# An expert's last half chunk of up columns as rounded columns beside their rests, and ScalarE rounding the gated products

## The chip, the cores and the metric

One core of a Trainium2 chip. The metric is the device time of one execution in microseconds (us), the median of several runs.

## What is computed

64 x 64 rows of 512 numbers (4096 tokens) are mapped by one of 8 subject matrices, and the result x goes through a layer of eight experts and a shared one. Cut to what matters here:

```
h1 = einsum('nc,efc->enf', x, expert_fc1)      # 8 experts, 352 hidden, C = 512
h2 = einsum('nc,efc->enf', x, expert_fc2)
h  = silu(h1) * h2
out_e = einsum('enf,ecf->enc', h, expert_proj)
y = combine (two experts per token) of out_e
y = y + sigmoid(x @ shared_gate_w.T) * ((silu(s1) * s2) @ shared_proj.T)   # 1408 hidden
return x_in + y
```

All of it is 32-bit. The kernel gets its accuracy from three passes of rounded operands: a number is split into a rounded part (hi, type fp32r) and the rest (lo = raw - hi, rounded too), and a product is hi*hi + hi*lo + lo*hi.

## The kernel before

Tokens come in tiles of 128. A first stretch (up to some 413 us) maps the tokens, runs five of the eleven shared chunks on blocks of 512 tokens and computes the routing. A last stretch (from some 896 us) runs the other six shared chunks and adds everything up. Between them lie the experts, 39 steps (XT): 32 *whole* tiles of 256 gathered tokens and 7 *single* tiles of 128. The step after a single is always a whole tile and is written together with it (`single_and_whole`, 7 times, whole tiles with a plain stage order but another queue order on VectorE and ScalarE). Of the other 25 whole tiles the first has an order of its own (`gate_first`, `hidden_first`), the last is done together with the preparation of the last stretch, and 23 go through `whole_step`; I call those plain.

A whole tile on TensorE (PE), lines 1003 to 1055:
- Stage 1: three chunks of hidden units, FCH = 128, 128 and 96 wide. For chunk j `whole_chunk` runs the gate half (h = 0) and the up half (h = 1) over KC = 4 slices of C, three passes of 256 columns each: 24 passes, 72 in all. Both halves go to `bank_h[j]`, columns 0 to 255 and 256 to 511. PE starts chunk j when `ex.h_mul` says that the bank of the tile before is read.
- Stage 2, `expert_stage2` (L1024): PE waits for `ex.h_lo` to reach 3i+2 (the rests of chunks 0 and 1), runs 12 passes of 512 columns with eight transposes of the next tile's rows in between, waits for 3i+3 (chunk 2) and runs 6 passes.

```
for ks in ((0, 1), (2,)):
    pe.wait_ge(ex.h_lo, 3 * i + ks[-1] + 1)
    for r in range(2):
```

Beside it, in queues that each engine works through in the written order:
- ScalarE (ACT), `whole_step` L1321: per chunk two roundings of the next expert's weight pieces (`w_hi`, `wp_hi`; 7 pieces a tile), then the silu of the gate half (`expert_gate`, L1316, to `g_sb`); then the roundings `x_hi` of the next tile, and `keep_y` copies of `bank_o`.
- VectorE (DVE), `whole_step` L1749: per chunk the rests of the two weight pieces (`split_w`, L1743, to `w_lo`, `wp_lo`), then `hidden` (L1619): product of up half and `g_sb` into `h_sb` (L1623, `ex.h_mul`), rounding to `h_hi` (L1625), rest to `h_lo` (L1627, `ex.h_lo`); at the end the rests `x_lo` of the next tile (`rest_x`, L1633). PE starts the next stage 1 when `ex.x_lo` and the `ex.w_lo` of the four up pieces are there.
- SP loads an expert's weights two steps ahead, once all rests of the tile's pieces are done (`next_load`).

```
def hidden(f, n, j, fn, width, bank2, tok):
    dve.wait_ge(f.g_ready, n + 1)
    ... tensor_tensor(h_sb, bank2, g_sb, ALU.mult).then_inc(f.h_mul, 1)
    dve.wait_ge(f.h_mul, n + 1)
    ... tensor_copy(h_hi, h_sb).then_inc(f.h_hi, 1)
    dve.wait_ge(f.h_hi, n + 1)
    ... tensor_tensor(h_lo, h_sb, h_hi, ALU.subtract).then_inc(f.h_lo, 1)
```

Of the kernel before, what the change touches and what calls it, by code (L numbers as in the profile page):

```python
# [108 lines left out]
def build_program(nc, x, subj, cond_w, gates, ew12, ewp, sw12, swp, consts, out):  # L109
# [10 lines left out]
    with ctx:  # L120
# [675 lines left out]
        def _(pe):  # L796
# [258 lines left out]
            def single_up(i):  # L1055

                pe.wait_ge(ex.x_lo, 2 * (i + 1))
                pe.wait_ge(ex.w_lo, PIECES * i + KC)
                for h in range(2):
                    for k in range(KC):  # L1060
                        a = k * 2 * F + h * F

                        def small(pas, at=3 * k):
                            q = at + pas
                            if h == 0 and q < 2 * KC:
# [23 lines left out]
            def single_and_whole(i, g, loaded, loaded_next):  # L1089
# [103 lines left out]
        def _(act):  # L1193
# [253 lines left out]
        def _(dve):  # L1447
# [171 lines left out]
            def hidden(f, n, j, fn, width, bank2, tok):  # L1619
# [357 lines left out]
```

## Time and profile before

| | us |
|---|---|
| median of 3 runs (lowest, highest) | 1267.74 (1266.4, 1268.84) |
| profiled execution, its own time | 1266.22 |
| its span, first to last instruction | 1264.2 |
| PE busy | 1247.4 |
| DVE busy | 866.7 |
| ACT busy | 488.5 |

A busy PE is not PE at its peak, since passes overlap and their ends are modelled. The time of a pass is read from the distance of the starts, or from the chain of waits, which puts passes end to end.

### The profile page before, as it was taken

How to read it: one execution, taken by the hardware profiler on the slowest of the kernel's cores; microseconds unless marked ns; L12 is line 12 of the kernel's file. 1: busy time of each engine (PE TensorE's matmuls, PEld its weight loads, DVE VectorE, ACT ScalarE, POOL GpSimd, SP SyncE). 2: the span in 40 equal slices, each digit the busy share in tenths (PEclk: the TensorE clock that was granted, in tenths of full speed). 3: DMA queues.
4: the chain of work that ended last, by engine and by line, in shares of the span. 5: the costliest groups of instructions: out<-in, count | busy, mean ns of one | idle time of the engine just before them, and what ended most of it. 6: DMA issues, size and time to landing. Idle time of an engine off the chain costs nothing.

```text
span 1264.2 us, 20269 instructions
## 1 busy us (share of the span) xinstructions
PE 1247.4 (99%) x7006; PEld 1075.0 (85%) x7006; DVE 866.7 (69%) x1414; ACT 488.5 (39%) x821; POOL 292.3 (23%) x395
## 2 busy tenths in 40 slices
PE   7999999999999999999999999999999999999998
PEld 5788888888888999999999999999887787887887
DVE  4544554459654787787787777778778778778675
ACT  4322232221011566666666665556313314213211
POOL 3267874000001121221221222110231130030110
PEclk9999999999999999999999999999999999999999
DMA  8488887202215678678678686784796785885842
GB/s 302 143 295 293 292 311 250 91 35 100 100 57 189 227 268 293 220 267 290 221 269 288 220 281 219 263 293 161 268 352 199 274 258 168 290 250 175 289 136 100
DMA packets 110670, 284.29 MB, mean 225 GB/s; under 512 B 11570, under 2 KB 11698, under 8 KB 104850
## 3 DMA queue, kind: packets, MB, share of 16 engines
q1 hardware_dynamic: 73410, 186.51, 40.9%
q0 software_dynamic: 13872, 54.27, 13.8%
q10 hardware_dynamic: 23328, 42.74, 10.2%
q8 instruction: 34, 0.56, 0.2%
q14 instruction: 26, 0.21, 0.0%
HBM read 217.16 MB, written 66.32 MB: 224 GB/s over the span
## 4 chain that ended last, share of the span: by engine, by line
PE 92%; DMA 3%; DVE 3%; ACT 1%; issue 1%; SPq 1%; DVEq 0%; ACTq 0%
PE bank_h L870 43%; PE bank_o L870 27%; PE bank_h L1132 9%; PE bank_t L1132 6%; PE bank_t L860 2%; PE bank_t L870 2%; PE bank_t L811 1%; DMA rawp<-ewp 1%; PE bank_o L821 1%; DMA w_early<-late_up 1%; DMA rawp<-swp 1%; DMA x_lo<-late_up 0%; PE bank_h L821 0%; PE bank_h L803 0%; DVE rawp L1840 0%
## 5 line engine op out<-in xcount | busy, mean ns | idle before, releaser
L870 PE MATMUL bank_h<-x_hi,w_hi 128*128 128x256 f32 (+2 forms) x1096 | 348.7, 318 | 0.3 <-DVE x_lo L1633 0.3
L870 PE MATMUL bank_h<-x_hi,w_lo 128*128 128x256 f32 (+2 forms) x1096 | 342.7, 313 | 0.0
L870 PE MATMUL bank_h<-x_lo,w_hi 128*128 128x256 f32 (+2 forms) x1096 | 341.9, 312 | 0.0
L870 PEld LDWEIGHTS bank_h<-x_hi,w_lo 128*128 128x128 f32 (+1 forms) x1096 | 200.2, 183 | 12.6
L870 PEld LDWEIGHTS bank_h<-x_hi,w_hi 128*128 128x128 f32 (+1 forms) x1096 | 200.3, 183 | 12.2 <-issue 0.9
L870 PEld LDWEIGHTS bank_h<-x_lo,w_hi 128*128 128x128 f32 (+1 forms) x1096 | 200.3, 183 | 11.2
L870 PE MATMUL bank_o<-wp_hi,h_hi 128*128 128x512 f32 (+1 forms) x502 | 204.9, 408 | 0.1
L870 PE MATMUL bank_o<-wp_lo,h_hi 128*128 128x512 f32 (+1 forms) x502 | 203.9, 406 | 0.0
L870 PE MATMUL bank_o<-wp_hi,h_lo 128*128 128x512 f32 (+1 forms) x502 | 202.7, 404 | 0.0
L1743 DVE TENSOR_TENSOR w_lo<-raw,w_hi 128x704 fp32r<-128x704 f32 x156 | 132.4, 885 | 56.7 <-ACT w_hi L1194 56.7
L1194 ACT ACTIVATE w_hi<-raw 128x704 fp32r<-128x704 f32 (+1 forms) x168 | 126.7, 802 | 8.9 <-DMA rawp<-swp 6.4
L756 POOL COPY idx_stage<-token_of 128x2 int32 (+3 forms) x39 | 9.8, 251 | 496.4 <-PE bank_t L860 321.6
L1240 ACT ACTIVATE g_sb<-bank_h 128x512 f32<-128x512 f32 x40 | 23.9, 598 | 243.4 <-PE bank_h L870 243.4
L870 PEld LDWEIGHTS bank_o<-wp_hi,h_lo 128*128 128x128 f32 (+1 forms) x502 | 94.3, 188 | 22.7
L870 PEld LDWEIGHTS bank_o<-wp_lo,h_hi 128*128 128x128 f32 (+1 forms) x502 | 94.6, 188 | 21.0
L870 PEld LDWEIGHTS bank_o<-wp_hi,h_hi 128*128 128x128 f32 (+1 forms) x502 | 94.6, 188 | 18.9 <-DVE h_lo L1627 0.8
L1623 DVE TENSOR_TENSOR h_sb<-bank_h,g_sb 96x256 f32<-96x256 f32 (+1 forms) x136 | 67.9, 499 | 59.8 <-ACT g_sb L1240 37.5
L760 POOL DMA_INDIRECT rows<-xf_rows,idx_stage x71 | 86.7, 1221 | 59.4 <-issue 59.4
L1461 DVE COPY xt<-bank_t 128x512 f32<-128x512 f32 x28 | 19.3, 690 | 90.3 <-PE bank_t L811 72.8
L1319 ACT ACTIVATE g_sb<-bank_h 128x256 f32<-128x256 f32 (+1 forms) x96 | 36.8, 383 | 110.2 <-PE bank_h L870 110.2
L781 POOL DMA_INDIRECT rows<-slot_rows,slot_of x32 | 32.3, 1009 | 190.1 <-DVE res L1840 121.5
L860 PE MATMUL bank_t<-cst,rows 128*128 128x128 f32 x284 | 75.8, 271 | 0.0
(238 smaller groups left out, 2169.8 us busy)
## 6 DMA issues: line engine op xcount, KB each, us to landing
raw<-ew SPq DMA_DIRECT2D x39, 1408.0 KB, 7.4
rawp<-ewp SPq DMA_DIRECT2D x39, 512.0 KB, 8.0
w_early<-late_up ACTq DMA_DIRECT2D x69, 256.0 KB, 3.9
slot_rows<-res SPq DMA_DIRECT2D x32, 512.0 KB, 4.1
x_hi<-late_up ACTq DMA_DIRECT2D x46, 256.0 KB, 3.9
x_lo<-late_up ACTq DMA_DIRECT2D x46, 256.0 KB, 3.1
xt_in<-xf_transposed SPq DMA_DIRECT2D x11, 1024.0 KB, 7.7
late_up<-raw POOLq DMA_DIRECT2D x6, 1792.0 KB, 7.9
```

Of the source, the lines that this page charges most:

```text
L760: pool.indirect_dma_start(rows[:, s, :], None, xf_dram, bass.IndirectOffsetOnAxis(idx_stage[:, s:s + 1].bitcast(U32), 0),).then_inc(ex.row ...
L781: pool.indirect_dma_start(picks[u][:, k, :], None, slot_dram, bass.IndirectOffsetOnAxis(slot_of[:, k, t:t + 1].bitcast(U32), 0),).then_inc ...
L811: m = pe.transpose(bank[:, c * P:(c + 1) * P], rows[:, k % 4, c * P:(c + 1) * P], ident)
L860: m = pe.transpose(bank_t[r % 2][:, k * P:(k + 1) * P], source[:, k * P:(k + 1) * P], ident)
L870: mm = pe.matmul(dst, a, m, start=(first and i == 0), stop=(last and i == 2))
L1132: m = pe.matmul(bank[:, :], halves[w][:, k, :], x2[x][:, k, :], start=(first and k == 0 and i == 0), stop=(k == 1 and i == 2), skip_group_ ...
L1194: copy = lambda o, i: nc.scalar.activation(o, i, ACT.Copy)
L1240: nc.scalar.activation(g_sb[:, (j % 2) * BN:(j % 2 + 1) * BN], bank_h[2 * (j % 2)][:, :], ACT.Silu).then_inc(f.g_ready, 1)
L1319: nc.scalar.activation(g_sb[0:fn, j * TS:(j + 1) * TS], bank_h[j][0:fn, 0:TS], ACT.Silu).then_inc(ex.g_ready, 1)
L1461: nc.vector.tensor_copy(xt[:, k % 2, :, :], bank[:, :].rearrange("p (k t) -> p k t", k=KC)).then_inc(fxt_ready, 1)
L1623: nc.vector.tensor_tensor(h_sb[0:fn, g], bank2, g_sb[0:fn, g], ALU.mult).then_inc(f.h_mul, 1)
L1743: nc.vector.tensor_tensor(lo, raw, hi, ALU.subtract).then_inc(ex.w_lo, 1)
```

## The change

An expert's up columns are stored in another order, so that the last 64 of a row are the ones that are treated in a new way. In `w12_hi` each slice now has 64 columns more (`E_HI = 2 * F + FOLD`): behind the rounded last 64 columns lie *their rests*. One stationary operand of 128 columns is thus 64 rounded columns beside their 64 rests. Two passes, one with x_hi and one with x_lo, give in partitions 0 to 63 hi*x_hi + hi*x_lo and in 64 to 127 lo*x_hi + lo*x_lo; their sum is the product. That takes 2 passes for a slice and not 3, and 17 for a slice over the tile and not 18. The 32 up columns of chunk 2 that are left ride in the gate half, whose stationary operand grows from 96 to 128 columns; they come out in partitions 96 to 127 of the bank's first half.

For chunk 2 ScalarE therefore copies partitions 64 to 127 of the up half to `u_sb[0:64]`, does the silu, and copies partitions 96 to 127 of the gate half to `u_sb[64:96]`. VectorE adds the other 64 partitions to `u_sb[0:64]` and multiplies `u_sb` and `g_sb`. The weight rests have 640 columns for the four up pieces, and one instruction (4x64 columns) writes the folded rests, counted by `ex.w_lo`, so all waits on it go by RESTS = 8 a tile in place of 7. A single tile still runs three passes over all columns and multiplies in two instructions (32 and 320 columns).

In plain tiles and the first, ScalarE rounds the gated products (`expert_h_hi`), not VectorE. In plain tiles it rounds chunk j-1 behind the gate of chunk j, and VectorE subtracts chunk j-1 behind the product of chunk j; in the first tile both come behind the same chunk's product. In the 7 whole tiles beside a single, and in the last, VectorE does all three as before.

```diff
+FOLD = 64
+E_HI = 2 * F + FOLD
+UP_AT = F + FCH[2][1] - FOLD
+FOLD_AT = 2 * F - FOLD
...
+        u_sb = h_sb[:, 3 * TS:4 * TS]
...
+        RESTS = PIECES + 1
+
+        def folded_piece(u):
+
+            raw = raw12[:, u * E_UP:(u + 1) * E_UP].rearrange("p (k f) -> p k f", k=KC)
+            hi = w12_hi[:, u * KC * E_HI:(u + 1) * KC * E_HI].rearrange("p (k f) -> p k f", k=KC)
+            return raw[:, :, FOLD_AT:2 * F], hi[:, :, FOLD_AT:2 * F], hi[:, :, 2 * F:E_HI]
...
+                bank = bank_h[j][:, h * TS:(h + 1) * TS]
+                if (j, h) == (2, 1):
+                    for part, x in enumerate((ex_x_hi, ex_x_lo)):
+                        m = pe.matmul(bank, w12_hi[:, hi + FOLD_AT:hi + E_HI], x[:, k, :], start=(start and part == 0),
+                                      stop=(stop and part == 1))
+                    return m
+                f = FCH[j][0] + h * UP_AT
+                return product(bank, (w12_hi[:, hi + f:hi + f + P], w12_lo[:, lo + f:lo + f + P]),
...
             def whole_chunk(i, u, j):
                 at_least(pe, ex.h_mul, 3 * (i - 1) + j + 1)
+                if j == 2:
+                    pe.wait_ge(ex.w_lo, RESTS * i + KC + 1)
...
             def expert_gate(i, j):
                 fn = FCH[j][1]
                 act.wait_ge(ex.h_full, 3 * i + j + 1)
-                nc.scalar.activation(g_sb[0:fn, j * TS:(j + 1) * TS], bank_h[j][0:fn, 0:TS], ACT.Silu).then_inc(ex.g_ready, 1)
+                if j == 2:
+                    copy(u_sb[0:FOLD, :], bank_h[2][FOLD:P, TS:2 * TS])
+                gate = nc.scalar.activation(g_sb[0:fn, j * TS:(j + 1) * TS], bank_h[j][0:fn, 0:TS], ACT.Silu)
+                if j == 2:
+                    gate = copy(u_sb[FOLD:fn, :], bank_h[2][fn:P, 0:TS])
+                gate.then_inc(ex.g_ready, 1)
+
+            def expert_h_hi(i, j):
+                fn = FCH[j][1]
+                act.wait_ge(ex.h_mul, 3 * i + j + 1)
+                copy(h_hi[0:fn, j, 0:TS], h_sb[0:fn, j * TS:(j + 1) * TS]).then_inc(ex.h_hi, 1)
...
                     if not gate_first:
                         expert_gate(i, j)
+                        if j:
+                            expert_h_hi(i, j - 1)
+                if not gate_first:
+                    expert_h_hi(i, 2)
...
+            def expert_gated(i, j):
+                fn = FCH[j][1]
+                up = bank_h[j][:, TS:2 * TS]
+                if j == 2:
+                    dve.wait_ge(ex.g_ready, 3 * i + 3)
+                    nc.vector.tensor_tensor(u_sb[0:FOLD, :], up[0:FOLD, :], u_sb[0:FOLD, :], ALU.add).then_inc(ex.u_ready, 1)
+                    dve.wait_ge(ex.u_ready, i + 1)
+                    up = u_sb[0:fn, :]
+                gated(ex, 3 * i + j, j, fn, TS, up, j)
...
             def whole_step(i, u, hidden_first=False, row_tiles=2):
                 for j in range(3):
                     if hidden_first:
-                        expert_hidden(i, j)
-                    split_w(i + 1, 1 - u, (2 * j, 2 * j + 1))
+                        expert_gated(i, j)
+                        expert_rest(i, j)
+                    split_w(i + 1, 1 - u, (2 * j, 2 * j + 1), row_tiles == 1)
                     if not hidden_first:
-                        expert_hidden(i, j)
+                        expert_gated(i, j)
+                        if j:
+                            expert_rest(i, j - 1)
+                if not hidden_first:
+                    expert_rest(i, 2)
```

Where instructions stand, as the built program has them, each with its line, its tiles and what it waits for. First VectorE in a plain tile, from the product of chunk 1 (`bank_h1`) to the rests of chunk 2; before:

```order
L1623 TENSOR_TENSOR h_sb<-bank_h1,g_sb 128x256 [waits ex_g_ready]
L1625 CAST h_hi<-h_sb 128x256 [waits ex_h_mul]
L1627 TENSOR_TENSOR h_lo<-h_sb,h_hi 128x256 [waits ex_h_hi]
L1742 REGISTER_ALU
L1743 TENSOR_TENSOR wp_lo<-rawp,wp_hi 128x512 [waits ex_w_hi]
L1742 REGISTER_ALU
L1743 TENSOR_TENSOR wp_lo<-rawp,wp_hi 128x512 [waits ex_w_hi]
L1622 REGISTER_ALU
L1623 TENSOR_TENSOR h_sb<-bank_h2,g_sb 96x256 [waits ex_g_ready]
L1625 CAST h_hi<-h_sb 96x256 [waits ex_h_mul]
L1627 TENSOR_TENSOR h_lo<-h_sb,h_hi 96x256 [waits ex_h_hi]
```

and now:

```order
L1663 TENSOR_TENSOR h_sb<-bank_h1,g_sb 128x256 [waits ex_g_ready]
L1675 TENSOR_TENSOR h_lo<-h_sb,h_hi 128x256 [waits ex_h_hi]
L1796 REGISTER_ALU
L1799 TENSOR_TENSOR wp_lo<-rawp,wp_hi 128x512 [waits ex_w_hi]
L1796 REGISTER_ALU
L1799 TENSOR_TENSOR wp_lo<-rawp,wp_hi 128x512 [waits ex_w_hi]
L1808 REGISTER_ALU
L1809 TENSOR_TENSOR h_sb<-bank_h2,h_sb 64x256 [waits ex_g_ready]
L1663 TENSOR_TENSOR h_sb<-h_sb,g_sb 96x256 [waits ex_g_ready,ex_u_ready]
L1675 TENSOR_TENSOR h_lo<-h_sb,h_hi 128x256 [waits ex_h_hi]
L1675 TENSOR_TENSOR h_lo<-h_sb,h_hi 96x256 [waits ex_h_hi]
```

The roundings (CAST) are gone. The rest of chunk 1 (the last row but one, 128x256), which stood right behind chunk 1's product, now stands behind the sum (64x256) and the product (96x256) of chunk 2; in its old place is the rest of chunk 0.

ScalarE in the same plain tile, from the gate of chunk 1 to the first x rounding; before:

```order
L1319 ACTIVATE g_sb<-bank_h1 128x256 [waits ex_h_full]
L1194 ACTIVATE wp_hi<-rawp 128x512 x2
L1318 REGISTER_ALU
L1319 ACTIVATE g_sb<-bank_h2 96x256 [waits ex_h_full]
L1222 ISA
L1194 ACTIVATE x_hi<-bank_t0 128x4x128 [waits ex_t_done]
```

and now:

```order
L1346 ACTIVATE g_sb<-bank_h1 128x256 [waits ex_h_full]
L1219 ACTIVATE h_hi<-h_sb 128x256 [waits ex_h_mul]
L1219 ACTIVATE wp_hi<-rawp 128x512 x2
L1343 REGISTER_ALU
L1219 ACTIVATE h_sb<-bank_h2 64x256 [waits ex_h_full]
L1346 ACTIVATE g_sb<-bank_h2 96x256
L1219 ACTIVATE h_sb<-bank_h2 32x256
L1219 ACTIVATE h_hi<-h_sb 128x256 [waits ex_h_mul]
L1219 ACTIVATE h_hi<-h_sb 96x256 [waits ex_h_mul]
L1247 ISA
L1219 ACTIVATE x_hi<-bank_t0 128x4x128 [waits ex_t_done]
```

Chunk 2 has three instructions behind `ex_h_full` where it had one, and the roundings of chunks 1 and 2 follow them.

PE in the same tile, at the end of stage 1 (`bank_h2`) and the start of stage 2 (`bank_o0`); before:

```order
L870 MATMUL bank_h2<-x_hi,w12_hi 96x256
L870 MATMUL bank_h2<-x_lo,w12_hi 96x256
L870 MATMUL bank_h2<-x_hi,w12_lo 96x256
L1052 REGISTER_ALU
L1026 REGISTER_ALU [waits ex_rows0]
L1031 ISA [waits ex_o_kept,ex_w_lo]
L870 MATMUL bank_o0<-wp_hi,h_hi 128x512 [waits ex_h_lo]
```

and now:

```order
L1027 MATMUL bank_h2<-x_lo,w12_hi 128x256
L1027 MATMUL bank_h2<-x_hi,w12_hi 128x256
L1027 MATMUL bank_h2<-x_lo,w12_hi 128x256
L1027 MATMUL bank_h2<-x_hi,w12_hi 128x256
L1027 MATMUL bank_h2<-x_lo,w12_hi 128x256
L1077 REGISTER_ALU
L1051 REGISTER_ALU [waits ex_rows0]
L1056 ISA [waits ex_o_kept,ex_w_lo]
L887 MATMUL bank_o0<-wp_hi,h_hi 128x512 [waits ex_h_lo]
```

The passes of the up half alternate x_hi and x_lo over one stationary operand, 8 in all where there were 12. What PE asks for ahead of the first pass of stage 2 is what it asked for before. In the whole tile beside a single, VectorE has the sum ahead of chunk 2's product, rounding and rest, then two weight rests of 640 columns, the folded rest (4x64), and then the two x rests.

## Rows read from the trace of the kernel before

**Rows 1.** The page's engines: busy us (share of the span) and instructions.
```profile
PE 1247.4 (99%) x7006; PEld 1075.0 (85%) x7006; DVE 866.7 (69%) x1414; ACT 488.5 (39%) x821; POOL 292.3 (23%) x395
```
**Rows 2.** The page's chain that ended last, share of the span by engine.
```profile
PE 92%; DMA 3%; DVE 3%; ACT 1%; issue 1%; SPq 1%; DVEq 0%; ACTq 0%
```
**Rows 3.** Timeline of PE (start us, us, instruction): stage 1 to stage 2.
```profile
658.71 0.28 PE L870 MATMUL bank_h<-x_hi,w_lo 128*96 128x256 f32 x1
658.83 0.39 PE L870 MATMUL bank_o<-wp_hi,h_hi 128*128 128x512 f32 x1
```
**Rows 4.** Chain in order of time (start us, us, what): stage 1 of that tile.
```profile
650.44 8.55 PE bank_h L870 x72
```
**Rows 5.** Timeline of ACT, same tile: chunk 1, weight pieces, chunk 2.
```profile
656.19 0.39 ACT L1319 ACTIVATE g_sb<-bank_h 128x256 f32<-128x256 f32 x1 [1.11 <-PE bank_h L870]
656.47 1.14 ACT L1194 ACTIVATE wp_hi<-rawp 128x512 fp32r<-128x512 f32 x2
659.03 0.38 ACT L1319 ACTIVATE g_sb<-bank_h 96x256 f32<-96x256 f32 x1 [1.41 <-PE bank_h L870]
```
**Rows 6.** Timeline of DVE, same tile: chunk 0's rest, chunk 2.
```profile
654.55 0.42 DVE L1627 TENSOR_TENSOR h_lo<-h_sb,h_hi 128x256 fp32r<-128x256 f32 x1
654.89 1.69 DVE L1743 TENSOR_TENSOR w_lo<-raw,w_hi 128x704 fp32r<-128x704 f32 x2
...
659.44 0.42 DVE L1623 TENSOR_TENSOR h_sb<-bank_h,g_sb 96x256 f32<-96x256 f32 x1 [0.42 <-ACT g_sb L1319]
659.89 0.29 DVE L1625 CAST h_hi<-h_sb 96x256 fp32r<-96x256 f32 x1
```
**Rows 7.** Groups by line and form (busy us, mean ns), DVE, then ACT.
```profile
L1627 DVE TENSOR_TENSOR h_lo<-h_sb,h_hi 128x256 fp32r<-128x256 f32 x64 | 27.2, 425 | 2.2
...
L1623 DVE TENSOR_TENSOR h_sb<-bank_h,g_sb 128x256 f32<-128x256 f32 x64 | 27.1, 423 | 12.3 <-ACT g_sb L1319 11.0
...
L1194 ACT ACTIVATE wp_hi<-rawp 128x512 fp32r<-128x512 f32 x83 | 47.6, 621 | 6.2 <-PE bank_o L870 6.2
```
**Rows 8.** Timeline of DVE and PE: stage 1 after a single's neighbour.
```profile
744.22 1.28 DVE L1633 TENSOR_TENSOR x_lo<-bank_t,x_hi 128x512 fp32r<-128x512 f32 x2
...
745.05 0.39 PE L870 MATMUL bank_o<-wp_hi,h_lo 96*128 96x512 f32 x1
745.75 0.38 PE L870 MATMUL bank_h<-x_hi,w_hi 128*128 128x256 f32 x1 [0.31 <-DVE x_lo L1633]
```
**Rows 9.** Timeline of DVE and PE: the last whole tile's stage 2.
```profile
890.43 0.42 DVE L1627 TENSOR_TENSOR h_lo<-h_sb,h_hi 128x256 fp32r<-128x256 f32 x1
...
890.61 0.28 PE L870 MATMUL bank_h<-x_hi,w_lo 128*96 128x256 f32 x1
891.00 0.47 PE L870 MATMUL bank_o<-wp_hi,h_hi 128*128 128x512 f32 x1
```
**Rows 10.** Timeline of PE and DVE: stage 2 beside a single.
```profile
645.22 0.39 PE L870 MATMUL bank_o<-wp_hi,h_hi 128*128 128x512 f32 x1
...
648.89 0.40 PE L870 MATMUL bank_o<-wp_hi,h_hi 96*128 96x512 f32 x1
...
650.28 0.28 PE L870 MATMUL bank_h<-x_hi,w_hi 128*128 128x256 f32 x1
...
646.96 1.68 DVE L1743 TENSOR_TENSOR w_lo<-raw,w_hi 128x704 fp32r<-128x704 f32 x2
648.56 1.28 DVE L1633 TENSOR_TENSOR x_lo<-bank_t,x_hi 128x512 fp32r<-128x512 f32 x2
```
**Rows 11.** Busy time by stretch: us, PE, PEld, DVE, ACT, POOL, clock, DMA share, GB/s.
```profile
30.00:34.00 4.00, 2.08 (x13) 1.72 (x12) 3.27 (x6) 1.81 (x3) 1.78 (x4) 1.00 0.90 345
...
658.83:663.89 5.06, 5.06 (x29) 4.07 (x27) 3.30 (x7) 2.50 (x5) 1.10 (x2) 1.00 0.57 212
```
**Rows 12.** Timeline of PE: the wait in the first stretch.
```profile
33.38 0.47 PE L870 MATMUL bank_t<-w_hi,wp_hi 128*128 128x512 f32 x1 [1.92 <-DVE w_lo L1471]
```

More of the change, by code:

```diff
@@ L1004, in up_product @@
             def up_product(i, u, j, h, k, start, stop):
-                f0, fn = FCH[j]
-                a = u * E_UP + k * 2 * F + h * F + f0
-                return product(bank_h[j][0:fn, h * TS:(h + 1) * TS], (w12_hi[:, a:a + fn], w12_lo[:, a:a + fn]),
+                lo, hi = expert_up(u, k)
+                bank = bank_h[j][:, h * TS:(h + 1) * TS]
[6 more added lines that the diff above has]
+                return product(bank, (w12_hi[:, hi + f:hi + f + P], w12_lo[:, lo + f:lo + f + P]),
                                (ex_x_hi[:, k, :], ex_x_lo[:, k, :]), start, stop)
@@ L1325, in whole_step @@
                         expert_gate(i, j)
+                        expert_h_hi(i, j)
                     if j == 0:
@@ L1617, in slot_tokens, with gated @@
                 nc.vector.tensor_copy(token_of[:, :], tok_f[:, :]).then_inc(routing_done, 1)
-            def hidden(f, n, j, fn, width, bank2, tok):
+            def gated(f, n, j, fn, width, bank2, tok):
                 g = slice(tok * width, (tok + 1) * width)
@@ L1628, in hidden @@
                                         ).then_inc(f.h_lo, 1)
+            def hidden(f, n, j, fn, width, bank2, tok):
+                gated(f, n, j, fn, width, bank2, tok)
+                rounded(f, n, j, fn, width, tok)
+                hidden_rest(f, n, j, fn, width, tok)
             def rest_x(f, n, r):
@@ L1736, in _, with split_w @@
             hiddens(0, BLOCKS - 1, between=steps_of({0: slot_tokens}))
-            def split_w(i, u, part):
+            def split_w(i, u, part, single=False):
                 pieces = list(expert_pieces(u))
@@ L1742, in split_w, with expert_rest @@
                     dve.wait_ge(ex.w_hi, PIECES * i + k + 1)
-                    nc.vector.tensor_tensor(lo, raw, hi, ALU.subtract).then_inc(ex.w_lo, 1)
+                    if k < KC and not single:
+                        raw, hi, lo = (a[:, 0:FOLD_AT] for a in (raw, hi, lo))
+                    nc.vector.tensor_tensor(lo, raw, hi, ALU.subtract).then_inc(ex.w_lo, 2 if single and k == KC - 1 else 1)
+                    if k == KC - 1 and not single:
+                        raw, hi, lo = folded_piece(u)
+                        nc.vector.tensor_tensor(lo, raw, hi, ALU.subtract).then_inc(ex.w_lo, 1)
+            def expert_gated(i, j):
[7 more added lines that the diff above has]
+                gated(ex, 3 * i + j, j, fn, TS, up, j)
+            def expert_rest(i, j):
+                hidden_rest(ex, 3 * i + j, j, FCH[j][1], TS, j)
             def expert_hidden(i, j):
-                fn = FCH[j][1]
-                hidden(ex, 3 * i + j, j, fn, TS, bank_h[j][0:fn, TS:2 * TS], j)
+                expert_gated(i, j)
+                rounded(ex, 3 * i + j, j, FCH[j][1], TS, j)
+                expert_rest(i, j)
             def whole_step(i, u, hidden_first=False, row_tiles=2):
@@ L1772, in single_and_whole @@
                 dve.wait_ge(ex.h_full, 3 * (i + 1))
-                nc.vector.tensor_tensor(h_sb[:, 0:F], bank_h[2][:, 0:F], g_sb[:, 0:F], ALU.mult).then_inc(ex.h_mul, 3)
+                back = UP_AT - F
+                nc.vector.tensor_tensor(h_sb[:, F - back:F], bank_h[2][:, 0:back], g_sb[:, F - back:F], ALU.mult
+                                        ).then_inc(ex.u_ready, 1)
+                nc.vector.tensor_tensor(h_sb[:, 0:F - back], bank_h[2][:, back:F], g_sb[:, 0:F - back], ALU.mult
+                                        ).then_inc(ex.h_mul, 3)
                 split_w(i + 1, 1, (2, 3))
```

34 lines of the change are left out of this document (22 added, 12 removed).

## The prediction

> **What bounds the kernel now.** I read the page's engine table first: PE is busy for 99% of the span, VectorE (DVE) for 69% [rows 1]. The chain that ended last runs over PE for 92% [rows 2]. So any pass taken from PE counts in full, and any new wait of PE counts in full too. I then read the timeline of one plain whole tile. Stage 1 is 72 passes of 256 columns that take 8.55 us, 0.119 us each [rows 4]. Stage 2 follows with no gap: the last pass of chunk 2 starts at 658.71, the first of stage 2 at 658.83 [rows 3]. Before the change this works because VectorE finishes the hidden rests of chunks 0 and 1 (rounding and rest) while PE is still in stage 1; the rest of chunk 1 is issued ahead of the two 512-column weight rests, which are ahead of chunk 2's product. Only chunk 2's own rest comes late, and stage 2 asks for it only after its first 12 passes.
>
> **Passes removed.** The up half of chunk 2 needs 8 passes in place of 12. With 32 whole tiles that is 128 passes x 0.119 us = 15.2 us less on PE. The 20 remaining passes of chunk 2 grow from 96 to 128 stationary columns; chunks 0 and 1 already run 128 at the same 0.119 us on average over the tile, so I cost this at nothing (at most 0.4 us in all, if a 96-column pass were 0.0005 us shorter).
>
> **The wait added.** This is the main term. The order rows of VectorE show the rest of chunk 1 (128x256, waiting for ex_h_hi) now behind chunk 2's sum and chunk 2's product, and both of these wait for ScalarE (ACT), which waits for PE's last pass of chunk 2. PE's next instruction, the first pass of stage 2, waits for ex_h_lo at the count that this same rest of chunk 1 gives. PE does its work in order, so nothing else of PE fills the time. What I add up, from T, the moment at which PE would start stage 2 (658.83 in the tile read):
> - ScalarE sees the bank full at T+0.20 (659.03 against 658.83) [rows 3, 5]. Then three instructions in place of one: the copy of 64 partitions, the silu, the copy of 32 partitions. One of 256 columns out of a bank takes 0.38 us and lets the next start after 0.28 [rows 5]. The last ends at T+0.20+0.28+0.28+0.38 = T+1.14.
> - VectorE starts 0.03 later (659.44 after 659.41) [rows 5, 6], at T+1.17. The sum (64x256) is followed by the product after 0.45, as product and rounding follow each other now (659.44, 659.89): T+1.62. The rest of chunk 1 waits for nothing new and starts 0.34 later (654.55, 654.89): T+1.96. It takes 0.42 and ends at T+2.38 [rows 6].
> - ScalarE's rounding of chunk 1, which that rest needs, starts behind the three at about T+1.04. At a length between 0.38 (256 columns from a bank) and 0.62 (512 from SBUF) [rows 5, 7] it is done by T+1.7, before VectorE asks. Nothing for it.
> - PE starts again after the rest has landed. Two places show the price: after an x rest that ended at 745.50 PE started at 745.75, and its first pass took 0.10 longer than usual (0.38, not 0.28): 0.35 us [rows 8]. After the rest that ended at 890.85 it started at 891.00 with 0.08 more (0.47, not 0.39): 0.23 us [rows 9]. I take 0.30.
>
> So PE stands still for 2.38 + 0.30 = 2.7 us in each plain tile. There are 23: the 32 whole tiles without the 7 that share a step with a single, the first (its rests stay in place) and the last (all done by VectorE as before). 23 x 2.7 = **62.1 us**. Bounds: if ScalarE's two added copies cost only some 0.11 each in place of 0.28 and the restart 0.15, it is 2.2 us, 50.6 in all. If none of the six instructions overlaps its neighbour (0.10 more for two on ScalarE and for one on VectorE) and the restart is 0.35, it is 3.1 us, 71.3 in all.
>
> The product of chunk 2 reads SBUF where it read a bank. The rows say the same length for both, 425 ns for a 256-column subtraction in SBUF and 423 ns for the product out of a bank [rows 7]. The Trainium skill, VectorE: DVE Perf Modes, the section on the TRN2 errata, gives a bank source 62 cycles more than an SBUF source, 0.065 us; by it the sum would be 1.5 us lower (23 tiles), as an estimate from that page. The rows disagree, and I follow them.
>
> **Chunk 2's own rest in a plain tile.** ScalarE rounds it after the product (T+2.04), VectorE subtracts by about T+2.9. PE wants it 12 passes and 8 transposes after its restart, 3.67 us later (645.22 to 648.89) [rows 10]. Hidden, with 3 us to spare. The x rests behind it keep their distance to stage 2, because PE's transposes move with the stall.
>
> **The 7 whole tiles that share a step with a single.** There VectorE still does product, rounding and rest together, the rest of chunk 1 is long done, and stage 2 starts on time. But the rests of the next x tile wait in the same queue. Before: they start at 648.56, take 1.28 and end at 649.84, 4.62 after T = 645.22; PE needs them at 650.28, 5.06 after T [rows 10]. After: T+1.17 sum, +1.62 product, +2.07 rounding, +2.40 rest, +2.74 free. Two weight rests of 640 columns at 0.73 each (704 columns have 0.80: 646.96 to 648.56 for two, less some 1 ns a column), +4.20. The folded rest of 4x64 columns 0.34, +4.54. Two x rests 1.28, +5.82. With the restart of 0.35 PE starts stage 1 at T+6.2 and not T+5.06: 1.1 us, 7.7 us over seven; one of them already pays 0.5 now (745.75 in place of 745.28) [rows 8]. **+7.2 us**, between 4 (0.6 each) and 11 (1.6 each).
>
> **The rest.** The last whole tile starts stage 2 when VectorE has the rest of chunk 1 ready, at 890.85, already a little late now [rows 9]; VectorE has a queue of its own there, so the 0.5 us saved on PE is lost: +0.5. In the first tile ScalarE's rounding now waits for VectorE's product ahead of the weight copies; +0.5 (0 to 1.5). The 32-column piece cut from the single's product lies under 12 passes. SP and the DMAs wait for the same count of weight rests, one more per tile, and a tile that takes longer gives loads more room. Nothing.
>
> **Sum.** Against the profiled execution: 1266.2 - 15.2 + 62.1 + 7.2 + 1.0 = **1321.3 us**. That execution lies 1.5 us under the median of the three runs (1267.7), within their spread, and I don't correct for it. Low end: 1266.2 - 15.2 + 50.6 + 4.0 = 1305.6. High end: 1266.2 - 14.8 + 71.3 + 11.0 + 2.0 = 1335.7. I take 1304 to 1338. A difference of 0.2% (2.5 us) is about what a measurement of this kernel can tell from none.
>
> **Rivals.**
> 1. *The stall is covered* (faster). If the rest of chunk 1 were ready when stage 1 ends, only the passes and the smaller terms would be left: 1266.2 - 15.2 + 7.2 + 1.0 = 1259.2. This decides below a stall of 0.3 us a tile (7.0 / 23). For it: VectorE has 31% idle time and the product of chunk 1 is long done. Against it: the queue is in order, and the order rows put the rest behind two instructions that need PE's last pass. 0.03.
> 2. *The clock falls in the stalls* (much slower). A PE that stands still for 2.7 us in every 16 could be given the lower level, 1.2 GHz, when it resumes. If stage 2 then ran at half speed, its 5.06 us [rows 11] would become 10.1: 23 x 5.06 = 116 us more, 1437. Against it: after PE stood still for 1.92 us at 33.38 the granted clock stayed 1.00, the upper level of 2.4 GHz, in that stretch with half its time idle [rows 11, 12]. For it: that happened once, and shorter, and no row shows 2.7 us again and again. 0.07. The Trainium skill, TensorE: Matmul & The Clock Gate, the section on HAM oscillation, says that waits between bursts can bring the clock down at each burst; by that rule this rival's time would hold; the one row that bears on it does not agree.
> 3. *Part of the chain overlaps or part of the added work lies elsewhere* (a stall of 0.4 to 2.1 us, 1267 to 1304): 0.03, of which 0.01 within 0.2% of now. Something longer than my bounds (1338 to 1400): 0.03.
> 4. *The change does not do what it says*: the order rows show 8 passes, three ScalarE instructions and the rest behind the product. No chance given.
>
> My forecast has 0.84. Faster by over 0.2%: 0.03. Within: 0.01. Slower: 0.96.
>
> **What would show it.** In the profile after: PE's waits should list bank_o against DVE h_lo with about 60 us over 23 times, longest near 2.8; ScalarE's copy, silu, copy start 0.28 apart; VectorE's sum, product and rest of chunk 1 directly behind them; bank_h against DVE x_lo with some 7 times 1 us; PE's count falls by 128, its busy time by about 15 us; the granted clock stays at 1.00. A list of PE's waits without h_lo would make the forecast wrong, and so would a clock under 1.00. If h_lo waits are there but near 2.0 or 3.5 us, the chain is right and a length in it is off.

## The result, and the profile after

The changed kernel takes **1350.15 us** (median of 4 runs, 1348.32 to 1352.87), the kernel before 1267.61 us on the same chip (1266.4 to 1268.84): a ratio of 1.0661, 95% interval 1.0647 to 1.0676. The forecast was 1321.3, range 1304 to 1338. Slower was right; the time lies 29 us above the forecast and 12 above the range. The profiled execution took 1348.32 us, its span 1346.3.

The page's engines, the slices of PE's busy share and granted clock, and the chain by engine:

```profile
PE 1265.1 (94%) x6878; PEld 1077.7 (80%) x6878; DVE 859.4 (64%) x1413; ACT 540.6 (40%) x957; POOL 298.6 (22%) x395
...
PE   7999999999998988988989888888999999999999
...
PEclk9999999999999999999999998999999999999999
...
PE 85%; DVE 6%; ACT 3%; issue 2%; DMA 2%; POOL 1%; POOLq 0%; SPq 0%; DVEq 0%; ACTq 0%
```

PE has 128 instructions fewer than in [rows 1], yet 17.7 us *more* busy time, where the forecast had some 15 less. Fewer passes take longer in sum, which points at the clock, but not by itself: in the run with the late rests alone (below, clock 1.00 and no fold) PE's busy time is 1253.8, 6.4 us over the kernel before with the same passes. The chain now runs over DVE and ACT for 9% of the span, where [rows 2] had 4%. Who PE waits for (us in total, times, longest us), where the kernel before had none of the first and one of 0.3 us of the second [rows 8]:

```profile
PE bank_o L887 <- DVE h_lo L1675: 57.9, 24, 2.6
PE bank_h L887 <- DVE x_lo L1686: 8.3, 8, 1.1
```

The stall of a plain tile, in the timelines of ACT, DVE and PE (start us, us, instruction, idle before it and its releaser). It answers to [rows 3, 5, 6]; T, the moment at which PE would start stage 2, is here 471.84, 0.12 behind the start of the last pass:

```profile
472.04 0.38 ACT L1219 ACTIVATE h_sb<-bank_h 64x256 f32<-64x256 f32 x1 [0.67 <-PE bank_h L1027]
472.43 0.38 ACT L1346 ACTIVATE g_sb<-bank_h 96x256 f32<-96x256 f32 x1
472.82 0.38 ACT L1219 ACTIVATE h_sb<-bank_h 32x256 f32<-32x256 f32 x1
473.22 0.42 ACT L1219 ACTIVATE h_hi<-h_sb 128x256 fp32r<-128x256 f32 x1
...
473.23 0.42 DVE L1809 TENSOR_TENSOR h_sb<-bank_h,h_sb 64x256 f32<-64x256 f32 x1 [1.05 <-ACT h_sb L1219]
473.68 0.42 DVE L1663 TENSOR_TENSOR h_sb<-h_sb,g_sb 96x256 f32<-96x256 f32 x1
474.02 0.98 DVE L1675 TENSOR_TENSOR h_lo<-h_sb,h_hi 128x256 fp32r<-128x256 f32 x2
...
471.72 0.28 PE L1027 MATMUL bank_h<-x_lo,w_hi 128*128 128x256 f32 x1
474.49 0.50 PE L887 MATMUL bank_o<-wp_hi,h_hi 128*128 128x512 f32 x1 [2.49 <-DVE h_lo L1675]
```

The chain is the forecast one, link by link: three ScalarE instructions, the sum, the product, chunk 1's rest (the first of the two under `h_lo`), PE. ScalarE's three stand 0.39 apart, not 0.28. PE starts 2.65 after T, and its first pass is 0.11 longer than usual (0.50 against 0.39): 2.76 us a tile. Of the 23 plain tiles 22 have this stop of 2.49 us; the first has 2.58.

The rest of the surprise is in PE's restarts. The identical stop of 2.49 us is followed in some tiles by a pass of 0.50 and in others by one of about 0.80. (A first pass of 0.50 does not yet say that the clock held: behind 854.27, 871.81 and 940.23 it falls up to 1 us later.)

```profile
474.49 0.50 PE L887 MATMUL bank_o<-wp_hi,h_hi 128*128 128x512 f32 x1 [2.49 <-DVE h_lo L1675]
490.46 0.79 PE L887 MATMUL bank_o<-wp_hi,h_hi 128*128 128x512 f32 x1 [2.49 <-DVE h_lo L1675]
...
854.27 0.50 PE L887 MATMUL bank_o<-wp_hi,h_hi 128*128 128x512 f32 x1 [2.49 <-DVE h_lo L1675]
871.81 0.50 PE L887 MATMUL bank_o<-wp_hi,h_hi 128*128 128x512 f32 x1 [2.49 <-DVE h_lo L1675]
...
924.26 0.50 PE L887 MATMUL bank_o<-wp_hi,h_hi 128*128 128x512 f32 x1 [2.49 <-DVE h_lo L1675]
940.23 0.50 PE L887 MATMUL bank_o<-wp_hi,h_hi 128*128 128x512 f32 x1 [2.49 <-DVE h_lo L1675]
```

The busy time by stretch shows why (columns as in [rows 11]; the clock is the third number from the end):

```profile
474.49:476.49 2.00, 2.00 (x11) 1.64 (x12) 0.42 (x1) 0.38 (x2) 0.00 (x0) 1.00 0.09 31
...
490.00:492.00 2.00, 1.53 (x5) 1.18 (x6) 0.83 (x3) 0.42 (x1) 0.00 (x0) 0.52 0.26 92
492.00:494.00 2.00, 2.00 (x8) 1.53 (x8) 0.00 (x0) 0.51 (x2) 0.18 (x1) 0.63 0.00 0
494.00:496.00 2.00, 2.00 (x10) 1.63 (x9) 1.29 (x2) 0.60 (x2) 0.99 (x2) 1.00 0.00 0
...
854.27:856.27 2.00, 2.00 (x9) 1.61 (x10) 0.42 (x1) 0.06 (x1) 0.00 (x0) 0.76 0.18 65
871.81:873.81 2.00, 2.00 (x7) 1.46 (x8) 0.42 (x1) 0.06 (x1) 0.00 (x0) 0.64 0.13 47
```

After the stop that ends at 474.49 the granted clock stays at 1.00, the level of 2.4 GHz. Around the one that ends at 490.46 it goes to 0.5, the level of 1.2 GHz, and comes back after nine slow passes. Stretch by stretch it falls in 14 places between 490 and 961, each at another of the 23 stops, one of them twice as long as the others; the mean over the run is 0.981. What a fall costs is read from the distance of two restarts in the last expert loop, all of it the same work: 940.23 - 924.26 = 15.97 us where the clock stayed up, 871.81 - 854.27 = 17.54 where it fell a moment after the restart. That is 1.6 us. Added up over the 14 places (1.4 to 1.6 each, 2.9 for the long one) it makes **22 us**.

### The profile page after: what moved, and what is told of

It is laid out like the page before. It is cut to its first block, busy times and chain, and to the rows that moved or that the text cites. A ratio compares the mean times of both kernels' runs of the same rounds, so it can differ in the third digit from the quotient of the medians.

```text
span 1346.3 us, 20218 instructions
## 1 busy us (share of the span) xinstructions
PE 1265.1 (94%) x6878; PEld 1077.7 (80%) x6878; DVE 859.4 (64%) x1413; ACT 540.6 (40%) x957; POOL 298.6 (22%) x395
## 4 chain that ended last, share of the span: by engine, by line
PE 85%; DVE 6%; ACT 3%; issue 2%; DMA 2%; POOL 1%; POOLq 0%; SPq 0%; DVEq 0%; ACTq 0%
PE bank_h L887 37%; PE bank_o L887 25%; PE bank_h L1157 8%; PE bank_t L1157 6%; PE bank_t L877 2%; PE bank_h L1027 2%; PE bank_t L887 2%; ACT h_sb L1219 2%; DVE h_sb L1663 1%; DVE h_sb L1809 1%; PE bank_t L828 1%; ACT g_sb L1346 1%; DMA rawp<-ewp 1%; DVE w_lo L1799 1%; DVE h_lo L1675 1%
## 5 line engine op out<-in xcount | busy, mean ns | idle before, releaser
L887 PE MATMUL bank_h<-x_hi,w_hi 128*128 128x256 f32 (+1 forms) x968 | 314.3, 325 | 8.3 <-DVE x_lo L1686 8.3
L887 PE MATMUL bank_h<-x_hi,w_lo 128*128 128x256 f32 (+1 forms) x968 | 307.5, 318 | 0.0
L887 PE MATMUL bank_h<-x_lo,w_hi 128*128 128x256 f32 (+1 forms) x968 | 307.3, 317 | 0.0
L887 PEld LDWEIGHTS bank_h<-x_hi,w_hi 128*128 128x128 f32 x968 | 184.3, 190 | 22.7 <-issue 10.4
L887 PEld LDWEIGHTS bank_h<-x_hi,w_lo 128*128 128x128 f32 x968 | 184.2, 190 | 12.6
L887 PEld LDWEIGHTS bank_h<-x_lo,w_hi 128*128 128x128 f32 x968 | 184.5, 191 | 10.8
L1799 DVE TENSOR_TENSOR w_lo<-raw,w_hi 128x640 fp32r<-128x640 f32 (+1 forms) x156 | 124.1, 831 | 59.7 <-ACT w_hi L1219 59.7
L1663 DVE TENSOR_TENSOR h_sb<-bank_h,g_sb 128x256 f32<-128x256 f32 (+1 forms) x104 | 54.5, 524 | 63.0 <-ACT g_sb L1265 37.5
L1686 DVE TENSOR_TENSOR x_lo<-bank_t,x_hi 128x512 fp32r<-128x512 f32 x64 | 42.7, 686 | 55.3 <-ACT x_hi L1219 55.3
L1799 DVE TENSOR_TENSOR wp_lo<-rawp,wp_hi 128x512 fp32r<-128x512 f32 (+1 forms) x117 | 75.8, 685 | 1.7
```

Source lines behind the costliest of these rows:

```text
L887: mm = pe.matmul(dst, a, m, start=(first and i == 0), stop=(last and i == 2))
L1663: nc.vector.tensor_tensor(h_sb[0:fn, g], bank2, g_sb[0:fn, g], ALU.mult).then_inc(f.h_mul, 1)
L1686: nc.vector.tensor_tensor(ex_x_lo[:, :, c], bank_t[r % 2][:, :].rearrange("p (k t) -> p k t", k=KC), ex_x_hi[:, :, c], ALU.subtract).then_ ...
L1799: nc.vector.tensor_tensor(lo, raw, hi, ALU.subtract).then_inc(ex.w_lo, 2 if single and k == KC - 1 else 1)
```

## The experiments

Before ran beside them at 1266.47, 1265.57 and 1266.63 us in three groups of runs, and each ratio is to the one of its group. The changed kernel was not run again in them; differences to its 1350.15 us cross groups, in which before's median moved by 2 us at most. Unless said otherwise an edit is made to the changed kernel.

**The fold alone.** VectorE does product, rounding and rest together in all tiles, ahead of the next chunk's weight rests.

```
 (VectorE)  split_w(i + 1, 1 - u, (2 * j, 2 * j + 1), row_tiles == 1)
-           expert_gated(i, j)
-           if j: expert_rest(i, j - 1)
+           expert_hidden(i, j)
 (ScalarE)  expert_gate(i, j)
-           if j: expert_h_hi(i, j - 1)
```

> The change with VectorE rounding and subtracting right behind each product, as in the kernel before; the fold alone. Theory A: 1257 to 1264, within 3 us of the version with the rest put first, as only VectorE's time differs (about 0.3 us more a chunk). Rival B (the fold costs): above 1300. Rival C (the rounding on ScalarE costs): this one is faster than the version with the rest put first by 5 us or more.

Measured: 1265.23 us (10 runs), ratio 0.9986, interval 0.9973 to 0.9998, clock 1.00. PE's waits:

```profile
PE bank_h L887 <- DVE x_lo L1681: 8.1, 8, 1.5
...
PE bank_o L887 <- DVE h_lo L1670: 1.3, 2, 0.8
```

The 85 us are not the fold's. But the fold gives almost nothing either: what it saves on PE it pays for in x_lo waits. The time lies 1 us above the range expected.

**The late rests alone.** The kernel before, no fold, but ScalarE rounds and both engines treat chunk j-1 behind chunk j.

```
 (VectorE)  split_w(i + 1, 1 - u, (2 * j, 2 * j + 1))
-           expert_hidden(i, j)
+           expert_gated(i, j)
+           if j: expert_rest(i, j - 1)
 (ScalarE)  expert_gate(i, j)
+           if j: expert_h_hi(i, j - 1)
```

> The kernel before with only the second half of the change: ScalarE rounds the gated products and VectorE subtracts a chunk later; no fold, 18 passes a slice. Theory A: stage 2 waits for silu (0.20 + 0.38), product (0.03 + 0.34) and rest (0.42 + about 0.1), 1.5 us in 23 tiles: 1266 + 34 = 1300 at full clock; up to 1330 if the clock falls after stops of 1.5 us as it does after 2.65. Rival B (the fold is what costs): within 3 us of the kernel before.

Measured: 1301.24 us (4 runs), ratio 1.0268, interval 1.0246 to 1.0290, clock 1.00.

```profile
PE bank_o L870 <- DVE h_lo L1650: 29.1, 24, 1.3
```

The order alone costs 35 us, with stops of 1.3 us, and the clock stays up. The fold's two copies and its sum (0.39 + 0.39 + 0.45 us) lengthen the stop to 2.49.

**The rest of the chunk before ahead of the next chunk's product**, and its rounding ahead of the next gate.

```
 (VectorE)  split_w(i + 1, 1 - u, (2 * j, 2 * j + 1), row_tiles == 1)
-           expert_gated(i, j)
            if j: expert_rest(i, j - 1)
+           expert_gated(i, j)
 (ScalarE)
-           expert_gate(i, j)
            if j: expert_h_hi(i, j - 1)
+           expert_gate(i, j)
```

> The change with one difference: in plain tiles VectorE subtracts chunk j-1 ahead of the sum and product of chunk j, and ScalarE rounds chunk j-1 ahead of the gate of chunk j. Fold, weight layout and the engine that rounds are kept. Theory A (the rest of chunk 1 behind chunk 2's product stops PE for 2.7 us in 23 tiles, and PE's clock falls in the wake of some of these stops): both terms go together, 1266.2 - 15.2 + 8 = 1259, between 1256 and 1263, PE waits for h_lo under 2 us in all, clock 1.00. Rival B (the fold itself is what costs: three ScalarE instructions, a sum, 128-column passes): the time stays above 1300. Rival C (ScalarE is too slow as the one that rounds): h_lo still waited for, above 1270.

Measured: 1276.27 us (4 runs), ratio 1.0079, interval 1.0051 to 1.0106, clock 1.00. 74 us are gone, but 17 more than expected are left. DVE and PE in a plain tile:

```profile
665.31 1.29 DVE L1799 TENSOR_TENSOR wp_lo<-rawp,wp_hi 128x512 fp32r<-128x512 f32 x2
666.52 0.42 DVE L1675 TENSOR_TENSOR h_lo<-h_sb,h_hi 128x256 fp32r<-128x256 f32 x1
...
666.45 0.28 PE L1027 MATMUL bank_h<-x_lo,w_hi 128*128 128x256 f32 x1
667.00 0.50 PE L887 MATMUL bank_o<-wp_hi,h_hi 128*128 128x512 f32 x1 [0.26 <-DVE h_lo L1675]
```

I had not looked at what else stands ahead of the rest: two 512-column weight rests. PE starts at 667.00 and not 666.57, with 0.11 on its first pass, 0.54 x 23 = 12 us. The other 5 lie in the sum expected, which is too low for the fold alone as well (1265). By the words of the two expectations rival C came true: h_lo is waited for 6.6 us, the time is above 1270, and the fold alone, where VectorE rounds, is 11 us faster. The rounding engine and the place in the queue differ together between these two runs; the next one separates them.

**The rest between the two weight pieces.**

```
 (VectorE)
-           split_w(i + 1, 1 - u, (2 * j, 2 * j + 1), row_tiles == 1)
-           expert_gated(i, j)
+           split_w(i + 1, 1 - u, (2 * j,), row_tiles == 1)
            if j: expert_rest(i, j - 1)
+           split_w(i + 1, 1 - u, (2 * j + 1,), row_tiles == 1)
+           expert_gated(i, j)
 (ScalarE)  likewise, with expert_h_hi(i, j - 1) between the pieces
```

> The changed kernel, but the rounding and the rest of the chunk before stand between the two weight pieces of a step on both engines, not behind the next chunk's gate or product. Theory (the stall is only the place of chunk 1's rest in VectorE's queue): with one 512-column weight rest ahead of it instead of two, the rest of chunk 1 ends some 0.3 us before PE asks, h_lo waits fall from 6.6 us (in the run with the rests first, whose rest stands behind both) to below 2, and the time is that of the fold done by VectorE alone, 1262 to 1267 us, clock 1.00. Rival (ScalarE's rounding costs PE something by itself, whatever the place): 1272 or more with h_lo waits of 5 us or more.

Measured: 1265.72 us (10 runs), ratio 1.0001, interval 0.9990 to 1.0012, clock 1.00; h_lo waits 0.5 us in all. It equals the fold alone, with ScalarE still rounding. So ScalarE's rounding costs nothing at this place, rival C is out, and the whole stall was one place in two queues.

**PE kept busy in the stop.** These runs leave the chain as it is and put passes of 256 columns, whose result nobody reads, between stage 1 and stage 2 of the plain tiles. They ask what the clock takes apart from the stop.

```
 (PE)  expert_stage1(i, u)
+      for _ in range(22):     # or 11, or 5
+          pe.matmul(bank_t[0][:, 0:TS], w12_hi[...], ex_x_hi[:, 0, :], start=True, stop=True)
       pe.wait_ge(ex.rows_loaded[1 - u], loaded)
```

> The change with 22 passes of 256 columns added on PE between stage 1 and stage 2 of the 23 plain tiles, into a bank that is overwritten later; nothing reads them. They take 22 x 0.119 = 2.6 us and so fill the stop of 2.65 us nearly to its end, and the chain that ends it is untouched. Theory A (the 25 us above the forecast are passes at the lower clock, because PE stood still): 1322 to 1327 and a clock of 1.00, though PE does 506 passes more. Rival D (the 25 us come from elsewhere, from transfers or from ScalarE or VectorE): 1346 to 1352, as the change, and the same for the clock.

> The changed kernel with 11 more passes of 256 columns between stage 1 and 2 of the 23 plain tiles (into a bank that nobody reads there), so that PE stands still for about 1.2 us there and not 2.5. The chain through ScalarE and VectorE keeps its length. Theory (only the long stop brings the clock down): clock 1.00, 1324 to 1330 us. Rival (what matters is that PE stops at all at this place, once a tile): clock near 0.98, 1345 to 1350.

> The same with 5 passes in place of 11, so that PE stands still for about 1.9 us in each plain tile. Time without a loss of clock: 1324 to 1330. Theory A (the stop must be near 2.5 us): clock 1.00 and that time. Theory B (a stop of 1.9 us is enough in some tiles): clock between 0.98 and 0.995 and 1331 to 1348, with stretches of 15 us at 0.9.

Measured, with the longest regular stop (PE's wait for h_lo in each plain tile):

| passes added | stop | time, us (runs) | clock |
|---|---|---|---|
| 22 | none | 1329.77 (4) | 0.999 |
| 11 | 1.18 us | 1328.37 (4) | 0.999 |
| 5 | 1.89 us | 1348.46 (4) | 0.983 |
| 0, the changed kernel | 2.49 us | 1350.15 (4) | 0.981 |

Stage 2 starts at the same distance from stage 1 in all four; 22 passes fill it:

```profile
471.05 0.28 PE L1027 MATMUL bank_h<-x_lo,w_hi 128*128 128x256 f32 x1
471.17 2.80 PE L1077 MATMUL bank_t<-x_hi,w_hi 128*128 128x256 f32 x22
473.83 0.50 PE L887 MATMUL bank_o<-wp_hi,h_hi 128*128 128x512 f32 x1
```

The time falls by 20 to 22 us although PE does *more*. That is the clock's share, and it agrees with the 22 us from the restarts. (With 22 passes the time is 3 us above the range expected. Its profile has one DMA wait of 2.8 us in the last stretch, at 984, and the only fall of its clock at it; its other executions, at a clock of 1.00, took as long, so the fall is not the reason. The 1.4 us between 22 and 11 passes are within their runs.) Between stops of 1.18 and 1.89 us the loss appears nearly whole: with 5 passes the clock falls in 13 places. With 11 it fell once in the expert loops, at 466, where waits of 0.77 and 1.51 us followed each other within 4 us. My theory A for 5 passes, that it takes a stop near 2.5, was wrong.

**Does a stop act alone?** The late rests only in every second plain tile, the other tiles with the rest between the weight pieces.

```
 (both engines)
+    late = (u == 1)      # the second run: u == 0
+    late: the changed kernel's order;  else: rest / rounding between the weight pieces
```

> The changed kernel's late rests only in the 12 plain tiles of buffer 1 (in a group the second of the two neighbours); in the other 11 the rest stands between the weight pieces, where PE does not stop. At full clock: 1265.7 + 12 x 2.76 = 1299 us. Theory A (each stop of 2.5 us can bring the clock down by itself): falls in about half of the 12 or more, clock 0.985 to 0.993, 1308 to 1320 us. Theory B (it takes a stop in the tile before as well, some 16 us earlier): clock 1.00 and 1296 to 1302.

> The mirror image: the late rests only in the 11 plain tiles of buffer 0 (in a group the first of the two neighbours, where the changed kernel never lost the clock). At full clock: 1265.7 + 11 x 2.76 = 1296 us. Theory A (each stop by itself): clock 0.985 to 0.995, 1302 to 1316. Theory B (a stop in the tile before is needed): clock 1.00, 1293 to 1299.

Measured: 1310.98 us (4 runs), ratio 1.0365, interval 1.0342 to 1.0389, clock 0.990; and 1307.12 us (4 runs), ratio 1.0320, interval 1.0299 to 1.0340, clock 0.990. Theory A in both: 8 falls in 12 stops and 8 in 11, and 12.1 / 8 = 1.5 and 11.0 / 8 = 1.4 us for each above the time at full clock (1265.72 + 2.76 for each of the 12 or 11 stops). PE's restarts in the first of the two:

```profile
489.11 0.79 PE L887 MATMUL bank_o<-wp_hi,h_hi 128*128 128x512 f32 x1 [2.49 <-DVE h_lo L1678]
...
541.13 0.50 PE L887 MATMUL bank_o<-wp_hi,h_hi 128*128 128x512 f32 x1 [2.49 <-DVE h_lo L1678]
...
591.71 0.79 PE L887 MATMUL bank_o<-wp_hi,h_hi 128*128 128x512 f32 x1 [2.49 <-DVE h_lo L1678]
...
827.24 0.79 PE L887 MATMUL bank_o<-wp_hi,h_hi 128*128 128x512 f32 x1 [2.49 <-DVE h_lo L1678]
857.94 0.79 PE L887 MATMUL bank_o<-wp_hi,h_hi 128*128 128x512 f32 x1 [2.49 <-DVE h_lo L1678]
```

Its stretches right behind the first three have a clock of 0.50, 1.00 and 0.50, and behind the last two 0.50. These two are 31 us apart, with no other wait of PE between them, so such stops still bring it down. And in the second run the first neighbour of a group, spared in every group of the changed kernel, is hit in every second one: it was not spared for its place in the program. What picks one of two identical stops was not tested.

**ScalarE's copies in place.** Why do the three instructions stand 0.39 apart?

```
-    copy(u_sb[0:FOLD, :], bank_h[2][FOLD:P, TS:2 * TS])
+    copy(u_sb[0:FOLD, :], bank_h[2][0:FOLD, TS:2 * TS])
-    gate = copy(u_sb[FOLD:fn, :], bank_h[2][fn:P, 0:TS])
+    gate = copy(u_sb[FOLD:fn, :], bank_h[2][FOLD:fn, 0:TS])
```

> The changed kernel, but ScalarE's two copies read the partitions that they write (0 to 63 and 64 to 95) instead of partitions 64 to 127 and 96 to 127, so the sum is made of other numbers than the up product: only the time counts. Theory A (the copies stand 0.39 apart from their neighbours because they move data to other partitions): the three instructions start 0.28 apart, chunk 2's chain is 0.22 shorter, 23 x 0.22 + 7 x 0.22 = 6.6 us less, 1341 to 1346 with the clock as it was. Theory B (the pitch comes from the number of partitions or the mix of copy and silu): pitch 0.39 again and 1347 to 1352.

Measured: 1347.84 us (4 runs), ratio 1.0634, interval 1.0610 to 1.0658. ACT:

```profile
476.33 0.38 ACT L1219 ACTIVATE h_sb<-bank_h 64x256 f32<-64x256 f32 x1 [0.67 <-PE bank_h L1027]
476.61 0.36 ACT L1346 ACTIVATE g_sb<-bank_h 96x256 f32<-96x256 f32 x1
476.99 0.38 ACT L1219 ACTIVATE h_sb<-bank_h 32x256 f32<-32x256 f32 x1
477.39 0.42 ACT L1219 ACTIVATE h_hi<-h_sb 128x256 fp32r<-128x256 f32 x1
```

Half of theory A. The first copy and the silu, now both reading and writing partitions from 0 on, stand 0.28 apart. The silu and the second copy, from 0 and from 64 on, stay 0.38 apart though neither moves data to other partitions. So the pitch goes with a change of the start partition from one instruction to the next, not with the move itself; that reading rests on these two pairs and was not varied further. The stop shrinks by 0.13 to 2.36 us, which would be 3 us for 23 tiles, but in the profiled execution the clock fell in 16 places of the expert loops and not in 14, and that takes it back: the time does not tell this run from the changed kernel.

**The x rests moved forward.** Beside a single tile they stood behind the weight rests of pieces 2 and 3 and the folded one. Here they stand behind piece 2's alone, and stage 1 asks for piece 3 when it comes to it.

```
 (VectorE)
-    split_w(i + 2, 0, (2, 3))
+    split_w(i + 2, 0, (2,))
     for r in range(2):
         rest_x(ex, 2 * (i + 2) + r, r)
-    split_w(i + 2, 0, range(KC, PIECES))
+    split_w(i + 2, 0, range(3, PIECES))
 (PE, expert_stage1)
-    pe.wait_ge(ex.w_lo, RESTS * i + KC)
+    pe.wait_ge(ex.w_lo, RESTS * i + KC - 1)      # RESTS * i + KC ahead of (j, h, k) == (0, 0, KC - 1)
```

It was run on the fold alone, and then together with the rest between the weight pieces:

> The fold with VectorE doing all of the hidden work (as in the run of the fold alone), and in the whole tile beside a single one the two x rests moved ahead of the weight rests of pieces 3 to 6, with stage 1 asking for piece 3 only at its fourth block of passes. Theory (the x rests stood behind too many weight rests, 8.1 us of bank_h against DVE x_lo over 7 times plus about 0.1 us restart each): that wait goes, 1265.2 - 8.8 = about 1256.5 us (1254 to 1260), DVE x_lo below 1 us in PE's waits, clock 1.00. Rival (the wait only moves, to the rest of weight piece 3 or to chunk 2's rests in that tile): 1263 to 1267, with 5 us or more of DVE w_lo or wp_lo in PE's waits.

> The changed kernel with two moves in the queues: the rest of the chunk before stands between the two weight pieces (as in the run of that name, 1265.7 us), and beside a single tile the x rests stand ahead of the weight rests from piece 3 on (as in the run that took 1258.2 with VectorE doing all hidden work). Theory (the two moves add up, and ScalarE's rounding neither gives nor costs anything): 1265.7 - 7.5 = 1258, within 2 us of the run with VectorE alone, DVE x_lo and h_lo together under 3 us in PE's waits. Rival (ScalarE's rounding makes VectorE early enough to remove more): 1253 or less.

Measured: 1258.24 us (6 runs), ratio 0.9937, interval 0.9921 to 0.9953; and **1257.01 us** (6 runs, 1254.59 to 1258.23), ratio 0.9925, interval 0.9909 to 0.9942, clock 1.00 in both. PE's waits in the second:

```profile
PE bank_h L1159 <- DVE raw L1945: 2.5, 4, 1.6
PE bank_h L887 <- DVE x_lo L1689: 1.2, 2, 0.9
...
PE bank_o L887 <- DVE h_lo L1678: 0.5, 1, 0.5
```

Both beat both kernels. Between them lies 1.2 us, with overlapping runs of two groups. Their plain tiles also show what the fold saves when nothing waits; the chain in order of time of the second:

```profile
807.24 7.20 PE bank_h L887 x60
814.44 0.96 PE bank_h L1027 x8
```

8.16 us for 68 passes, 0.120 each, against 8.55 for 72, 0.119 each [rows 4]. The fold saves 0.39 us a tile and not 0.48.

## Why the prediction was wrong

It failed at one step, the bound put on rival 2. The forecast's own sum held the clock at 1.00, gave the case of a fall 0.07, and priced it as all or nothing: 116 us or none. In its place the clock falls at 14 of the 23 stops, 22 us. Without that the execution would have taken about 1326, inside the range; the runs with 22 and 11 added passes, 1329.77 and 1328.37, show it. The main term, the stall, was right.

- **"Against it: after PE stood still for 1.92 us at 33.38 the granted clock stayed 1.00"** [rows 11, 12]. One stop that went well was taken for proof. In the changed kernel 9 of 23 stops of 2.5 us also went well. And the same wait does bring the clock down once in the traces here: with ScalarE's copies in place it was 3.13 us long, and the stretch behind it is at 0.59. With 5 added passes, the clock fell in 13 places with stops of 1.89 us, shorter than that row's. The rule named beside this rival (the Trainium skill, TensorE: Matmul & The Clock Gate, HAM oscillation, waits between bursts bring the clock down) was right in kind, though the section tells it of a kernel whose waits are longer than this stop. By its words at each burst it would have been 23 times; the traces show it at 14, and for part of stage 2 only. Half speed over all of stage 2, 5.06 us, was too much: 1.4 to 1.6 us is what one costs. The wait at 33.38 and the stretch behind it, in the run with the copies in place:

```profile
33.38 0.47 PE L887 MATMUL bank_t<-w_hi,wp_hi 128*128 128x512 f32 x1 [3.13 <-DVE w_lo L1511]
...
34.00:38.00 4.00, 4.00 (x12) 3.15 (x11) 2.92 (x5) 2.58 (x4) 0.83 (x4) 0.59 0.67 216
```

- **The stall**, 62.1 forecast: 23 x 2.76 = 63.5. Right in mechanism; nearly right in size by luck, since two errors cancel. ScalarE's pitch was 0.39 where I took 0.28 from a silu and a rounding that start on the same partition [rows 5]; the restart was 0.16 (0.05 to the start, 0.11 on the pass) where I took 0.30.
- **The passes**, -15.2 forecast: 32 x 0.39 = -12.5. The wrong sentence is that the growth of chunk 2 from 96 to 128 stationary columns costs at most 0.4 us in all. All 68 passes of the tile now have 0.120 where the 72 had 0.119. Part of it is the width (24 narrow passes took 2.83 us before, 0.118 each, by their starts from 833.20 on), but chunks 0 and 1, whose shape did not change, are some 0.001 longer a pass too. Why was not tested.
- **The x rests beside a single**, +7.2 forecast: +9.8. The waits are 8.3 us over 8 times, not 7: the tile behind the first also pays 0.93. Each costs 0.26 more than its wait (0.16 because the last pass's end in the trace lies behind the moment at which the next would start, 0.10 on the first pass), 10.4, less 0.6 that the kernel before paid already [rows 8]. Of each wait beside a single 0.22 is ScalarE's pitch (0.11 at two instructions), which the forecast lacked; that share is an estimate.
- **Last and first tile**, +1.0 forecast: +0.4 for the last; for the first what it pays is in the x rests.

The sum in measured terms: 1266.2 - 12.5 + 63.5 + 9.8 + 0.4 + 22 = 1349.4, against 1348.3. The experts also start 0.9 us earlier than before (411.83 against 412.77), which is most of what is left.
- **Rival 1** and the case of partial overlap did not occur: the queue is in order, and the rows of the order told so. VectorE's length for the product was the same from SBUF and from a bank (0.42), as the rows said.

## What to carry to other kernels

When a step is moved behind another in a queue, write down whom the consumer waits for at that moment, not the mean load: rests put one product later cost 35 us by themselves and, with the fold's longer chain, 63 us on the engine that bounds, though VectorE was idle a third of the time. Moving them to between two weight pieces, with the clock's share, took 84 us back. A saving on the bound engine gives its full worth only when what was just in time for the old, slower stage is moved forward too; here the fold gave 1 us until the x rests moved, then 7 to 10. And a stop on PE of about 2 us that comes again and again has a second price, the clock: take its chance from many stops, not from one, and price a fall by itself.

## What the runs showed that I had not expected

- Identical stops of PE of 2.49 us do and do not bring the clock to 1.2 GHz: 14 in 23 stops in the changed kernel (one of them 2.58 us), 8 in 12 and 8 in 11 when only every second tile stops. Stops of 1.89 us (one of 1.99): 13 in 23. Stops of 1.18 or 1.3 us once a tile: no fall at any of them, and one fall after waits of 0.77 and 1.51 us within 4 us. A fall costs 1.4 to 1.6 us.
- More work can be faster: 11 useless passes in each of 23 tiles, and the changed kernel is 22 us shorter.
- ScalarE's instructions of 256 columns start 0.28 us apart when both begin on partition 0, and 0.38 to 0.39 apart when their start partitions differ, in the pairs read here; nothing else was varied.
